# Where the two routers' transfers stand in their queues, and whether the second router copies its input

## The reference

```
x = x + 0.5 * moe(layernorm(x))        # 64 experts, 8 per token, at most 128 tokens per expert
x = x + attention(layernorm(x))        # 16 heads with 64 slots each, with decays
x = x + 0.5 * moe(layernorm(x))        # the same weights again
x = x + 0.5 * lut_ffn(layernorm(x))    # weights looked up in a table of 16 values
x = x + hgrn(layernorm(x))             # a linear recurrence over each sequence
x = x + 0.5 * lut_ffn(layernorm(x))
```

## Time and profile before

| | |
|---|---|
| median of 3 runs | 2971.13 us (2964.53 to 2974.62) |
| the profiled execution | 2975.17 us, its span 2973.5 us |
| busy of the span | TensorE 85%, weight load 72%, VectorE 59%, GpSimd 42%, ScalarE 30% |
| router 1 | about 7 to 120 us |
| experts 1 | about 125 to 375 us |
| attention | about 379 to 1938 us |
| router 2 | about 1943 to 2054 us |
| experts 2 | about 2059 to 2274 us |
| the rest | about 2274 to 2973.5 us |

### The profile page before, as it was taken

One profiled execution on the slowest core, in us unless ns is written; L12 is line 12 of the kernel. 1 busy time (PEld: TensorE's weight loads), 2 busy tenths in 40 slices (PEclk: granted clock), 3 DMA queues, 4 the chain that ended last, 5 costly groups with the idle time before them and its releaser, 6 DMA issues. The chain is left out here.

```text
span 2973.5 us, 46242 instructions
## 1 busy us (share of the span) xinstructions
PE 2515.5 (85%) x17244; PEld 2143.9 (72%) x17244; DVE 1756.3 (59%) x3538; ACT 890.2 (30%) x1886; POOL 1260.4 (42%) x1258
## 2 busy tenths in 40 slices
PE   6464579999999999999999999863654799796998
PEld 5343468888888888888888888753443688675787
DVE  5322248777777778777778878653222444364543
ACT  6222223333333333333333333252221222231322
POOL 2276724445555444455554444512884211242000
PEclk9988889999999999999999999955997899898999
DMA  6598700000000000000000000065995211111110
GB/s 225 149 239 222 162 18 7 13 12 15 16 5 12 15 15 12 9 12 15 15 5 14 13 15 8 3 213 153 220 215 116 64 46 47 40 57 47 36 33 31
DMA packets 211394, 190.57 MB, mean 64 GB/s; under 512 B 29200, under 2 KB 202224, under 8 KB 210672
## 3 DMA queue, kind: packets, MB, share of 16 engines
q1 hardware_dynamic: 182592, 140.29, 15.6%
q0 software_dynamic: 24576, 37.77, 6.8%
q10 hardware_dynamic: 4016, 9.70, 1.0%
HBM read 121.81 MB, written 65.88 MB: 63 GB/s over the span
## 5 line engine op out<-in xcount | busy, mean ns | idle before, releaser
L874 POOL TENSOR_TENSOR a_orstd<-a_ms,minus_half 128x8 f32<-128x8 f32 x64 | 106.3, 1660 | 636.8 <-DVE a_ms L1034 636.8
L1007 DVE TENSOR_TENSOR a_at<-a_psB,causal 128x384 f32<-128x384 f32 x512 | 260.3, 550 | 100.7 <-PE a_psB L1179 100.7
L854 POOL TENSOR_SCALAR a_pick<-a_index,lut_row 128x258 f32<-128x258 int32 x240 | 278.9, 1162 | 24.4
L601 PE MATMUL e_psX<-ident,e_xg 128*128 128x128 f32 x256 | 62.9, 333 | 193.8 <-DMA e_xg<-rows,slot_tok 193.6
L1027 DVE RECIPROCAL a_rz<-a_rz 128x256 f32<-128x256 f32 x128 | 221.4, 1731 | 0.0
L601 PEld LDWEIGHTS e_psX<-ident,e_xg 128*128 128x128 f32 x256 | 32.2, 161 | 241.0 <-DMA e_xg<-rows,slot_tok 236.5
L694 DVE TENSOR_TENSOR e_hT<-e_psH,e_sil 128x128 f32<-128x128 f32 x128 | 37.3, 291 | 272.9 <-ACT e_sil L662 272.9
L1557 DVE TENSOR_TENSOR f_hs<-f_psU,f_sil 128x512 f32<-128x512 f32 x96 | 66.2, 689 | 219.3 <-PE f_psU L1382 219.2
L857 POOL TENSOR_TENSOR a_found<-a_found,a_pick 128x258 f32<-128x258 f32 x240 | 177.4, 739 | 20.0
L1240 PE MATMUL a_psD<-a_v,a_at 128*128 128x128 f32 x1536 | 181.8, 275 | 0.0
L1240 PEld LDWEIGHTS a_psD<-a_v,a_at 128*128 128x128 f32 x1536 | 176.9, 192 | 0.1
(11 more groups left out here) (255 smaller groups left out, 7718.6 us busy)
## 6 DMA issues: line engine op xcount, KB each, us to landing
e_wg<-in_L_ffn_w_gate SPq DMA_DIRECT2D x128, 128.0 KB, 3.5
e_wu<-in_L_ffn_w_up SPq DMA_DIRECT2D x128, 128.0 KB, 3.7
e_wd<-in_L_ffn_w_down SPq DMA_DIRECT2D x128, 128.0 KB, 4.3
rows<-r_row SPq DMA_DIRECT2D x32, 320.0 KB, 3.1
stream_b<-r_zeros SPq DMA_DIRECT2D x22, 384.0 KB, 4.5
stream_a<-r_xt SPq DMA_DIRECT2D x32, 256.0 KB, 4.0
r_xt<-in_L_attn_hidden_states SPq DMA_DIRECT2D x16, 256.0 KB, 4.2
a_xab<-stream_a SPq DMA_DIRECT2D x16, 256.0 KB, 2.7
```

The costliest lines, as they stand in the source:

```text
L854: nc.gpsimd.tensor_scalar(pick[:, :, :], index[:, :, :], float(c), w["lut"][:, c:c + 1], ALU.is_equal, ALU.mult).then_inc(picked, 1)
L874: nc.gpsimd.tensor_tensor(out=flat(orstd[:, :, :]), in0=ms[:, :], in1=cst["minus_half"][:, 0:TT * HQ], op=ALU.pow).then_inc(orstd_ok, 1)
L1007: nc.vector.tensor_tensor(out=at[:, h, :], in0=psB[h % 2][:, 0:3 * P], in1=cst["causal"][:, :, :].rearrange("p a i -> p (a i)"), op=ALU.mu ...
```

## The change

`moe_router` gets `fresh`, the pair of streams, or nothing. With it (router 1) all eleven zero parts are issued directly behind the first loads and pads, the copies of iterations 0 to 3 stay in the loop (the next loads need their buffers), and the copies of iterations 4 to 7 come after the last read-backs. Without it (router 2) there are no copies and no zeros. In both, `counts_out` moves from SP's list to ScalarE's: the early counts after iteration 6's weights, the last after iteration 7's; `cum_out` becomes two semaphores. Router 2 needs no copy since the second experts add into `x_att` itself, attention's output, and into a third stream `stream_c`, which attention's SP fills with zeros, one tile of 128 rows in each of 32 transfers, DRAM to DRAM, from the zero pad of `rows`; two more transfers, behind the last store, fill the pads of `stream_c` and `x_att`.

```diff
                 load(0)
                 sp.dma_start(gw_in[:, :], gate_w).then_inc(gw_here, 16)
                 for j in range(1, R):
                     load(j)
-                sp.wait_ge(zero_set, 1)
...
-                for j in range(NJ):
-                    keep(j)
-                    for k in range(NZ * j // NJ, NZ * (j + 1) // NJ):
+                if fresh:
+                    sp.wait_ge(zero_set, 1)
+                    sp.dma_start(stream_a[NTOK:NTOK + P, :], zeros[:, 0:D]).then_inc(zero_out, 16)
+                    sp.dma_start(rows[NTOK:NTOK + P, :], zeros[:, 0:ROW]).then_inc(zero_out, 16)
+                    for k in range(NZ):
                         sp.dma_start(zv[:, k, :], zeros[:, :]).then_inc(zero_out, 16)
-                    sp.wait_ge(weights, 4 * j + 4)
-                    for u in range(2):
-                        sp.dma_start(rv[2 * j + u], row[:, j % R, u, :, :]).then_inc(row_out[j % R], 16)
+                for j in range(NJ - 1):
+                    if fresh and j < NJ - R:
+                        keep(j)
+                    rows_written(j)
                     if j + R < NJ:
                         load(j + R)
-                    if j == EARLY - 1:
-                        counts_out(0, 2 * EARLY)
                     if j == EARLY:
-                        sp.wait_ge(cum_out, 32)
+                        sp.wait_ge(cum_out[0], 32)
                         count_back(sp, QUARTERS, 0, 2 * EARLY)
-                counts_out(2 * EARLY, HALF)
-                sp.wait_ge(cum_out, 64)
+                rows_written(NJ - 1)
+                sp.wait_ge(cum_out[1], 32)
                 count_back(sp, QUARTERS[0:4], 2 * EARLY, HALF)
+                if fresh:
+                    for j in range(NJ - R, NJ):
+                        keep(j)
...
@@ block.scalar
                         for h in range(2):
                             nc.scalar.activation(row[:, j % R, u, h, D:ROW], ex[:, j % 2, u, h, :], ACT.Copy,
                                                  scale=rden[:, j % 2, 2 * u + h:2 * u + h + 1]).then_inc(weights, 1)
-                act.wait_ge(cum_out, 64)
+                    if j == EARLY:
+                        counts_out(0, 2 * EARLY)
+                counts_out(2 * EARLY, HALF)
+                act.wait_ge(cum_out[1], 32)
                 count_back(act, QUARTERS[4:8], 2 * EARLY, HALF)
...
@@ attention, block.sync
                 for b in range(B):
                     if b + 1 < B:
                         load(b + 1)
+                    for t in range(TT):
+                        at = (TT * b + t) * P
+                        sp.dma_start(second[at:at + P, :], zero_row).then_inc(zeroed, 16)
                     store_looked_up(b)
                     if b + 1 < B:
                         load_index(b + 1)
                     store(b)
+                for pad in (second, x_out):
+                    sp.dma_start(pad[NTOK:NTOK + P, :], zero_row).then_inc(zeroed, 16)
                 sp.wait_ge(x_out_done, 16 * B)
                 sp.wait_ge(looked_out, 48 * B)
+                sp.wait_ge(zeroed, 16 * (NTILE + 2))
...
@@ macaron
-        moe_router(nc, cst, "r2_", x_att, gate_w, rows, stream_a, stream_b, slot_tok, counts)
-        moe_experts(nc, cst, "e2_", rows, w_gate, w_up, w_down, slot_tok, stream_a, stream_b, pool_dma, 1)
+        moe_router(nc, cst, "r2_", x_att[0:NTOK, :], gate_w, rows, None, slot_tok, counts)
+        moe_experts(nc, cst, "e2_", rows, w_gate, w_up, w_down, slot_tok, x_att, stream_c, pool_dma, 1)
...
-        lut_ffn(nc, cst, "f1_", [stream_a, stream_b], x_ffn, wgT, wuT, wdT)
+        lut_ffn(nc, cst, "f1_", [x_att, stream_c], x_ffn, wgT, wuT, wdT)
```

More of the change, by code:

```diff
@@ L134, in constants, with moe_router @@
     return c
-def moe_router(nc, cst, tag, x_src, gate_w, rows, stream_a, stream_b, slot_tok, counts):
+def moe_router(nc, cst, tag, x_src, gate_w, rows, fresh, slot_tok, counts):
     HALF = NTILE // 2
@@ L151, in moe_router @@
         gwT = mem.sb("gwT", [P, DC, E])
-        zeros = mem.sb("zeros", [P, (NTOK // P + 1) * D // NZ])
+        zeros = mem.sb("zeros", [P, (NTOK // P + 1) * D // NZ]) if fresh else None
         xt = mem.sb("xt", [P, R, 2, 2, D])
@@ L218, in moe_router @@
         xv = x_src.rearrange("(h j p) d -> j p h d", h=2, p=P)
-        av = stream_a[0:NTOK, :].rearrange("(h j p) d -> j p h d", h=2, p=P)
         rv = rows[0:NTOK, :].rearrange("(h j p) d -> j p h d", h=2, p=P)
-        zv = stream_b.rearrange("(p k r) d -> p k (r d)", p=P, k=NZ)
+        if fresh:
+            stream_a, stream_b = fresh
+            av = stream_a[0:NTOK, :].rearrange("(h j p) d -> j p h d", h=2, p=P)
+            zv = stream_b.rearrange("(p k r) d -> p k (r d)", p=P, k=NZ)
         QUARTERS = [(f, h) for f in range(4) for h in range(2)]
@@ L238, in keep, with rows_written @@
                         sp.dma_start(av[2 * j + u], xt[:, j % R, u, :, :]).then_inc(x_kept[j % R], 16)
-                def counts_out(r0, r1):
+                def rows_written(j):
+                    sp.wait_ge(weights, 4 * j + 4)
                     for u in range(2):
-                        sp.wait_ge(keyed[u], r1 // 2)
-                    for h in range(2):
-                        sp.dma_start(by_half[h][:, r0 * P:r1 * P], cum[h * E:(h + 1) * E, r0 * P:r1 * P]).then_inc(cum_out, 16)
+                        sp.dma_start(rv[2 * j + u], row[:, j % R, u, :, :]).then_inc(row_out[j % R], 16)
                 load(0)
@@ L292, in turned_out, with counts_out @@
                         nc.scalar.activation(lnT[:, u, :, :], psT[u][:, :, :], ACT.Copy).then_inc(lnT_ok[u], 1)
+                def counts_out(r0, r1):
+                    for u in range(2):
+                        act.wait_ge(keyed[u], r1 // 2)
+                    for h in range(2):
+                        act.dma_start(by_half[h][:, r0 * P:r1 * P], cum[h * E:(h + 1) * E, r0 * P:r1 * P]).then_inc(cum_out[r0 > 0], 16)
                 act.wait_ge(gw_turned, DC)
@@ L332, in _ @@
             def _(pool):
-                nc.gpsimd.memset(zeros[:, :], 0.0).then_inc(zero_set, 1)
+                if fresh:
+                    nc.gpsimd.memset(zeros[:, :], 0.0).then_inc(zero_set, 1)
                 nc.gpsimd.tensor_copy(local[:, :, P], cst["tile_base"][:, 0:1].to_broadcast([P, NG])).then_inc(base_set, 1)
@@ L714, in attention_weights, with attention @@
     return w
-def attention(nc, cst, w, tag, stream_a, stream_b, x_out, indices, looked_up):
+def attention(nc, cst, w, tag, stream_a, stream_b, x_out, second, zero_row, indices, looked_up):
     HQ = 4
@@ L1859, in macaron @@
     stream_b = nc.dram_tensor("stream_b", [NTOK + P, D], F32, kind="Internal").ap()
-    x_att = nc.dram_tensor("x_att", [NTOK, D], F32, kind="Internal").ap()
+    x_att = nc.dram_tensor("x_att", [NTOK + P, D], F32, kind="Internal").ap()
+    stream_c = nc.dram_tensor("stream_c", [NTOK + P, D], F32, kind="Internal").ap()
     x_ffn = nc.dram_tensor("x_ffn", [NTOK, D], F32, kind="Internal").ap()
@@ L1873, in macaron @@
             w = attention_weights(nc, wmem, g_norm, lut)
-            moe_router(nc, cst, "r1_", x, gate_w, rows, stream_a, stream_b, slot_tok, counts)
+            moe_router(nc, cst, "r1_", x, gate_w, rows, (stream_a, stream_b), slot_tok, counts)
             wide = {name: [wmem.sb(f"w{name}_{part}", [P, cols], F32R) for part in ("high", "low")]
@@ L1888, in macaron @@
                 w[name] = [part[:, :].rearrange("p (c n) -> p c n", c=H if name == "o" else DC) for part in wide[name]]
-            attention(nc, cst, w, "a_", stream_a, stream_b, x_att, (gate_idx, up_idx, down_idx), looked_up)
+            attention(nc, cst, w, "a_", stream_a, stream_b, x_att, stream_c, rows[NTOK:NTOK + P, 0:D], (gate_idx, up_idx, down_idx), looked_up)
             clear_semaphores(nc, wmem)
-        moe_router(nc, cst, "r2_", x_att, gate_w, rows, stream_a, stream_b, slot_tok, counts)
-        moe_experts(nc, cst, "e2_", rows, w_gate, w_up, w_down, slot_tok, stream_a, stream_b, pool_dma, 1)
+        moe_router(nc, cst, "r2_", x_att[0:NTOK, :], gate_w, rows, None, slot_tok, counts)
+        moe_experts(nc, cst, "e2_", rows, w_gate, w_up, w_down, slot_tok, x_att, stream_c, pool_dma, 1)
         w_gu = [mem.sb(f"w_gu{k}", [P, FT, D]) for k in range(2)]
```

22 lines of the change are left out of this document (12 added, 10 removed).

## The result

| | before | changed |
|---|---|---|
| median | 2967.6 us | 2959.8 us |
| profiled execution | 2975.17 us, span 2973.5 | 2954.36 us, span 2952.5 |
| ratio of the times | | 0.9965 (0.9953 to 0.9978) |

Two of the changed kernel's 17 executions took 3387 and 4254 us at a granted clock of 0.75 and 0.64; the ratio leaves them out (the median of the other 15 is 2958.6). The ratio says 10 us faster, with 6.5 to 14 as the interval. I forecast 15.5 us faster and 2955, with 2945 to 2965.

A forecast was written before the change was run, and what follows sets the result against it. Bound: SP's late issue of the last counts delays each router's matmul behind the read-backs. Gains of 8.7 and 8.0 us, less 1.0 for attention and 0.2 for semaphores, make 15.5 off 2971.13: forecast 2955 us, range 2945 to 2965.

The forecast's parts named there:

- first link: Both routers' ends: last counts issued right after ScalarE's last weights, gaining 8.85 and 9.81 us by this alone.
- Second link: Both routers' ends: SP, free for the last read-backs at 81.6 and 2017.0, limits the gains to 8.3 and 6.9 us, low side.
- The term that failed: Both routers' ends: last read-backs to matmul kept at router 1's earlier 5.93 us (89.90 to 95.83).
- The early counts: Both routers: early counts, issued by ScalarE after iteration 6, take 0.6 us of issue and 5.1 us of landing.
- The cover: ScalarE's idling after iteration 6's weights, 2.73 us in router 1, hides two issues; router 2's 0.96 us may show up to 0.85.
- Zeros first: Router 1's front: 3.9 MB more zeros fill the empty DMA stretch from 20 to 30 us; cost nothing, bounds 0 and 3 us.
- the rival with a stall of 3 us: Router 1: the early zeros delay the load of iteration 4 by 3 us, giving 2958 us; chance 0.05.
- Copies last: Router 1's end: four copies (2 MB) behind the read-backs take 8 us and hide under 29 us of computing.
- Attention: Attention: 32 zeroing transfers hide; two pads behind the final store lose 1.0 us, bounds 0.2 and 2.5.
- Semaphores: One more semaphore in each router and in attention, 0.08 us each to clear, so 0.2 us lost.
- The last counts wait for the early read-backs: Both routers: last counts land only with the early read-backs; gains only 5.5 and 4.2 us, time 2962.6; chance 0.12.
- The scatters into x_att and stream_c: Second experts: scatters slower by over 1.4 us cost 32 us per further microsecond; 2991 us at 2.5 us; chance 0.04.

The follow-up runs named there:

- the second profile of before: The kernel before, unchanged, profiled once more: 21.0 and 20.2 us from ScalarE's last weights to the matmul behind the read-backs; first experts 244.2 us.

## Why the prediction was right in sign and range, and too large

*The change, first link* (the last counts' late issue, 8.85 and 9.81 us). The late issue was there, and the last counts even landed faster than taken: 3.7 and 4.2 us instead of 6.82 and 5.58. But it decided nothing alone. With the counts on ScalarE alone the lag fell by 0.3 to 0.9 us in router 1 and 0.4 to 1.5 in router 2.

*Second link* (SP's way to the last read-backs). I had SP free 7.4 and 8.5 us after ScalarE's last weights (81.6 and 2017.0) or sooner; it was free after 6.4 and 4.9. Right, on its better side.

*The term that failed* is "with 5.93 us from the last read-backs to the matmul". It was 91.02 - 79.56 = 11.5 us and 2011.17 - 2001.13 = 10.0. In the kernel before SP had just waited for the counts to land, and its queue had drained by then (a DMA share of 0.04 from 89 to 90 us); the 5.93 us were those of an empty queue. The change takes this wait away, so the last read-backs are issued while the early ones (768 KB) and the rows (640 KB) are still in flight. The runs with the rows behind, with 8 partitions and with the early counts sooner each take 1.5 us or more off the lag, and the last brings the term back to 6.4 and 5.9 us. I took a duration from a place where something else had made it short. That is 5.5 and 4.1 us; the other terms gave back 0.6 and 2.5 of these, and of 16.7 us forecast for the lags 10.2 came (3.8 and 6.4; 3.2 and 5.3 against the second profile of before). With the pads and semaphores taken off, the stages of the two pairs of profiles give 7 to 9 us, inside the ratio's 6.5 to 14.

*The number* came nearer than its working, and part of that is luck: it started from 2971.1, the median of three runs, and 17 runs have 2967.6. The 15.5 us taken off that would have been 2952, 8 us too low instead of 5.

*The early counts* were taken at 5.7 us from issue to SP's read-backs and took 7.4 (67.83 to 75.21) and 6.2 us (1990.16 to 1996.32). The cover that I had named for their issue was not quite enough in router 1, where the second one held ScalarE's queue until 70.35:

```profile
68.37 1.98 ACTq L303 DMA_DIRECT2D counts<-r_cum  x1
...
69.58 0.17 DVE L393 TENSOR_SCALAR r_nm<-r_mx 128x4 f32<-128x4 f32 x1
...
70.45 0.35 ACT L318 ACTIVATE r_ex<-r_lg,r_nm 128x64 f32<-128x64 f32 x1 [1.63 <-DVE r_nm L393]
```

VectorE had released the next exponentials at 69.75, so some 0.6 us were lost to the issue. The last weights ended 1.0 us earlier than before all the same.

*Zeros first*: as forecast. SP issues them and is free long before the rows of iteration 0, the stretch is full, and neither the rows nor the load of iteration 4 move (30.41 and 31.41 before):

```profile
12.96 10.39 SPq L258 DMA_DIRECT2D stream_b<-r_zeros  x11
23.39 2.00 SPq L242 DMA_DIRECT2D stream_a<-r_xt  x2
30.44 0.87 SPq L247 DMA_DIRECT2D rows<-r_row  x2
31.42 1.26 SPq L237 DMA_DIRECT2D r_xt<-in_L_attn_hidden_states  x2
```

```profile
20.00:30.00 10.00, 8.50 (x40) 7.59 (x40) 7.03 (x46) 5.67 (x19) 1.69 (x4) 1.00 0.92 362
```

VectorE begins iteration 4 at 37.79 instead of 37.76, so the rival with a stall of 3 us didn't come; the stretch moved 362 GB/s, not the 289 that I had taken.

*Copies last* cost nothing that shows: they are issued from 83.50 to 90.37, and the read-backs ahead of them take 7.6 us from the end of their issue to the matmul in router 1 and 7.5 in router 2, which has no copies. With the rows behind the read-backs too it is 9.3 against 7.5, so in that order up to 1.8 us may be theirs.

*Attention*: the zeroing hides. From the last store to router 2's first load it is 8.5 us with the pads behind the store, and 7.8, 6.8, 6.8 and 6.8 in the four traces with streams as before, 6.9 in the two with the pads at the start. So the pads cost 0.7 to 1.7 us, and 1.6 is nearer than the 1.0 taken. They land as transfers from DRAM to DRAM after 2.4 to 2.7 us, like the stores of the earlier trace rows:

```profile
L840 SPq DMA_DIRECT2D x_att<-rows x1: 598/598/598, 1921.0 to 1921.0; - x1
...
DMA to landing us min/median/max: 2.4/2.6/2.7
```

*Semaphores*: from the matmul to the first expert weight it is 29.02 to 29.03 and 29.31 to 29.32 us in the four traces whose routers have one `cum_out`, 29.09 to 29.10 and 29.37 to 29.39 in the eight that have two, at either granted clock. That agrees with the 0.08 us taken for one; these routers also differ in who issues the counts.

*The rivals.* "The last counts wait for the early read-backs" would have given 2962.6, nearer to the 2959.8 measured than my number, but not for its reason: in the changed kernel the last counts were issued before the early read-backs and landed in 3.7 and 4.2 us. A delay like the rival's is seen where the order is the other way round (7.6, 6.1 and 5.7 us in router 1 of three of the experiments), and it limits the better versions. The rule of the Trainium skill, page "DMA: Bandwidth & Descriptors", section "Queues, rings and completion order", that a completion waits for the engine's earlier writes agrees with this; that the engines simply share their time between the queues would look the same, and no run here separates the two. The scatters into x_att and stream_c landed as before, in 4.7 us at the median, and experts 2 took 219.7 us instead of 220.7 and 219.8 (to compare with the earlier trace rows):

```profile
L596 POOL DMA_INDIRECT x_att<-e_y,slot_tok x32: 1552/1591/1633, 2053.1 to 2247.7; - x32
L596 POOL DMA_INDIRECT stream_c<-e_y,slot_tok x32: 1552/1588/1593, 2056.4 to 2250.3; - x32
...
DMA to landing us min/median/max: 3.7/4.7/6.6
```

Not settled: why the counts on ScalarE alone measured 6 us when their lags give 1 to 2, and whether sharing or completion order delays the last counts.

## What to carry to other kernels

A duration from issue to landing belongs to the state of the queue in which it was measured: before it is used in a sum for a moved transfer, ask what the change puts ahead of it, above all where the change removes a wait that had let the queue drain. For a small transfer count the partitions, too: in router 1 the same 1 MB took 12.0 us from the last counts' landing to the matmul in transfers of 12 and then of 4 partitions, 9.1 us in transfers of 16; in router 2 it was 8.8 against 8.3.

## What the runs showed of the hardware

- Read-backs in 512-byte pieces: 66 GB/s with 0.25 of the engines busy when a transfer has 4 partitions, 152 GB/s with all busy when it has 16. With 8 partitions 0.50 were busy, at 155 GB/s in the last microsecond. The stretch that writes zeros in pieces of 3 KB moved 362 GB/s.
- A write of 256 KB of counts was through in 2.9 and 3.2 us alone, 4.3 and 4.1 us with 640 KB of rows in flight, and 5.7 to 6.7 us with 768 KB of read-backs issued ahead of it.
- The first experts, untouched, took 240 to 254 us from one profile to the next, 254 and 244 in two of one kernel: two single profiles can't be subtracted where a change of 10 us is looked for.
